# First period's rows from TensorE instead of DRAM, and the first slots regrouped by layer, in a CIN tower kernel

## The reference

```
x0 = e; xk = x0
for W in (W0, W1, W2):                       # W: (32, 32 or 64, 64)
    xk = relu(einsum('bmd,bhd,mhk->bkd', x0, xk, W))
    outs.append(sum(xk, axis=2))             # over d = 16
z = concatenate(outs, axis=1)                # (2048, 192)
h = relu(concatenate([z, dense_ctx]) @ W_top1 + b_top1)
h = relu(h @ W_top2 + b_top2)
y = h @ W_top3
```

## Time and profile before

| what | us |
|---|---|
| three timed runs, median | 655.9 |
| lowest and highest of them | 651.15, 657.07 |
| the profiled execution, own time | 651.37 |
| its span in the profile | 649.6 |

### The profile page before, as it was taken

One profiled execution on the slowest core, in us unless ns is written; L12 is line 12 of the kernel. 1 busy time (PEld: TensorE's weight loads), 2 busy tenths in 40 slices (PEclk: granted clock), 3 DMA queues, 4 the chain that ended last, 5 costly groups with the idle time before them and its releaser, 6 DMA issues.

```text
span 649.6 us, 7753 instructions
## 1 busy us (share of the span) xinstructions
PE 586.3 (90%) x2896; PEld 209.5 (32%) x2896; DVE 587.2 (90%) x327; ACT 358.4 (55%) x595; POOL 459.3 (71%) x381
## 2 busy tenths in 40 slices
PE   0078898999898989999999999999999999999997
PEld 0023332232232323333334323333334323333455
DVE  1038898999999999999999999999999999999993
ACT  0006382756646564757665465747576465736562
POOL 6676769588888888887989778887979692802020
PEclk9999999999999999999999999999999999999999
DMA  5285576728082644637280736546380816400000
GB/s 160 51 312 136 229 249 178 289 46 300 18 260 101 196 165 90 271 65 295 39 319 6 236 123 160 201 90 271 58 301 8 286 69 186 173 3 2 1 1 1
DMA packets 27137, 96.50 MB, mean 149 GB/s; under 512 B 7414, under 2 KB 12540, under 8 KB 22876
## 3 DMA queue, kind: packets, MB, share of 16 engines
q1 hardware_dynamic: 18908, 93.90, 43.2%
q0 software_dynamic: 8192, 2.11, 2.9%
HBM read 80.25 MB, written 15.73 MB: 148 GB/s over the span
## 4 chain that ended last, share of the span: by engine, by line
DVE 44%; PE 25%; issue 21%; POOL 4%; DMA 3%; SPq 1%; ACT 1%; another core or an unknown queue 0%; DVEq 0%; POOLq 0%
DVE prod L482 43%; PE acca L575 11%; PE accb L575 6%; PE acc L545 4%; POOL emb L361 3%; PE spread L616 2%; POOL prod L379 1%; SPq L279 1%; DMA emb<-in_table,idx 1%; DVE za L486 1%; DMA field_dram<-zb_field 1%; DMA rows<-field_dram 1%; DMA h<-in_w_swapped 0%; DVE zc L486 0%; PE spread L611 0%
## 5 line engine op out<-in xcount | busy, mean ns | idle before, releaser
L361 POOL DMA_INDIRECT emb<-in_table,idx x256 | 246.6, 963 | 82.2 <-issue 68.6
L575 PE MATMUL acca<-prod,w 128*64 128x512 f32 x1024 | 229.7, 594 | 4.1 <-DVE prod L482 2.8
L575 PE MATMUL accb<-prod,w 128*64 128x512 f32 x960 | 216.7, 596 | 15.9 <-DVE prod L482 12.0
L379 POOL TENSOR_TENSOR prod<-rows,mates 128x1024 f32<-128x1024 f32 x70 | 164.2, 2377 | 15.6 <-issue 15.2
L482 DVE TENSOR_TENSOR prod<-rows,x1a 128x2048 f32<-128x2048 f32 x64 | 145.9, 2282 | 5.4 <-PE acca L575 2.8
L482 DVE TENSOR_TENSOR prod<-rows,x1b 128x2048 f32<-128x2048 f32 x64 | 145.9, 2282 | 3.2 <-PE acca L575 1.9
L482 DVE TENSOR_TENSOR prod<-rows,x2b 128x2048 f32<-128x2048 f32 x64 | 145.9, 2282 | 1.3 <-remote 1.3
L482 DVE TENSOR_TENSOR prod<-rows,x2a 128x2048 f32<-128x2048 f32 x64 | 145.9, 2282 | 1.1 <-PE accb L575 0.8
L575 PEld LDWEIGHTS acca<-prod,w 128*64 128x64 f32 x1024 | 71.9, 137 | 147.0 <-issue 136.1
L575 PEld LDWEIGHTS accb<-prod,w 128*64 128x64 f32 x960 | 65.5, 137 | 158.6 <-issue 123.6
L709 ACT ACTIVATE x1a<-acc 64x512 f32<-64x512 f32 x62 | 35.3, 570 | 124.6 <-PE acc L545 103.4
(11 more groups left out here) (72 smaller groups left out, 251.4 us busy)
## 6 DMA issues: line engine op xcount, KB each, us to landing
rows<-field_dram SPq DMA_DIRECT2D x30, 2048.0 KB
field_dram<-zb_field SPq DMA_DIRECT2D x32, 256.0 KB
mates<-field_dram SPq DMA_DIRECT2D x16, 512.0 KB
emb<-in_table,idx POOLq DMA_INDIRECT x256
field_dram<-zb_field SPq DMA_DIRECT2D x32, 128.0 KB
field_dram<-zb_field SPq DMA_DIRECT2D x16, 192.0 KB
rows<-field_dram SPq DMA_DIRECT2D x2, 1024.0 KB
rows<-field_dram SPq DMA_DIRECT2D x1, 1536.0 KB
```

The source lines that it names most:

```text
L361: pool.indirect_dma_start(out=emb[q % EMBS][:, j * EMB:(j + 1) * EMB], out_offset=None, in_=table, in_offset=bass.IndirectOffsetOnAxis(ap= ...
L379: nc.gpsimd.tensor_tensor(prod0[:, (q * L0 + k) % RING0, :], rows[:, slot(q, t), :], mates[:, :], ALU.mult).then_inc(s_prod0p, 1)
L575: mm = nc.tensor.matmul(acc[j % 2][side * HID:(side + 1) * HID, :], (w1 if layer == 1 else w2)[:, step, :], prod[:, (made(layer, s, half, ...
```

## The change

Period 0 no longer goes through DRAM. VectorE first makes a pick matrix out of the identity (`pick`, in the space of `h2`). After the turn, ScalarE and VectorE copy the fields from PSUM into the lower 64 partitions of `field0`, and VectorE copies these to the upper 64. TensorE then forms the mates and each row tile by two matmuls (`pick_tile`), one for each half of the columns of the period, one from the lower and one from the upper 64 partitions; ScalarE copies them to `rows` and `mates` (VectorE half of the mates). Mates and tiles 0 to 4 come ahead of layer 0, tiles 5 to 7 behind it. The first five slots have new streams; slots 0 to 3 hold both subs of one layer of one period. In slots 0, 2 and 4 the last two units are made in halves. VectorE makes layer 0 of period 1 within slot 1, and the first two products of period 2 behind slot 2. The turns of periods 1 and 2, the sums of layer 0, GpSimd's gathers and the `keep_busy` calls are placed anew.

```diff
-    FIRST = [(0, 2), (2, 2), (4, 1), (5, 3)]
+    PICKED = [MATES, 0, 1, 2, 3, 4, 5, 6, 7]
+    EARLY = [[(1, 0), (1, 1)], [(2, 0), (2, 1)], [(1, 2), (1, 3)], [(2, 2), (2, 3)], [(1, 4), (1, 5)]]
     def streams(j):
-        if j == 0:
-            return [(1, 0), (1, 1)]
+        if j < len(EARLY):
+            return EARLY[j]
...
+    def feeds(j):
+        return j in (0, 2, 4)
     def vector_units(j):
         a, b = streams(j)
-        if 1 <= j < SUBS - 1:
+        if len(EARLY) < j < SUBS - 1:
             a, b = b, a
-        if j == 1:
+        if j in (1, 3, 5):
             return [(*stream, half, u) for half in range(2) for stream in (a, b) for u in range(UNITS)]
...
-    FIELDS_AT = {(0, 3): 2}
-    SUM0 = {}
+    FIELDS_AT = {(0, 0): 1, (0, 3): 2}
+    SUM0 = {(1, 1): [(k, 1) for k in range(L0)], (2, 3): [(k, 2) for k in range(L0)]}
-    def on_vector(q):
-        return q < 2
+    def on_vector(q, k):
+        return q < 2 or q == 2 and k < 2
...
 # SyncE
-            list_fields(0)
-            mates_in(0)
-            for g, (t, count) in enumerate(FIRST):
-                spread_rows(0, t, count, s_first[g])
 # GpSimd
-            gather_early(0)
+            gather(0, 0, GATHERS)
+            gather(1, 0, 2)
             pool.wait_ge(s_turned, 1)
-            gather_early(1)
-            pool.wait_ge(s_l0, L0)
-            gather_early(2)
-            gather_early(3)
+            gather(1, 2, 4)
+            pool.wait_ge(s_picked, 4)
+            gather(1, 6, 5)
+            pool.wait_ge(s_l0, 3)
+            gather(1, 11, 5)
+            gather(2, 0, 5)
+            pool.wait_ge(s_used, pairs_of(0, 0, 0))
+            gather(2, 5, 4)
+            pool.wait_ge(s_used, pairs_of(0, 0, 1))
+            gather(2, 9, 4)
+            pool.wait_ge(s_used, pairs_of(0, 1, 0))
+            gather(2, 13, 3)
+            gather(3, 0, STRETCH)
             halve12(0)
...
-            for k in range(L0):
+            gather(4, 0, STRETCH)
+            for k in range(2, L0):
                 product0(2, k)
...
 # VectorE
+            for c in range(2):
+                for j, count, half, first, step, times in LIST_PARTS:
+                    part = c * HID * P + c * HID + half * FIELDS + 2 * j + c
+                    ones_of = bass.AP(ident[:, :].tensor, part, [[P, HID], [0, times], [2, count]])
+                    to = bass.AP(h2[:, :, :].tensor, c * HID * TOP2 * 2 + 8 * first, [[TOP2 * 2, HID], [8 * step, times], [1, count]])
+                    last = nc.vector.tensor_scalar_max(to, ones_of, 0.0)
+            dve.wait_ge(s_turned, 1)
+            for d in (2, 3):
+                for f in range(2):
+                    last = nc.vector.tensor_copy(field0_at(f, d), turned_at(f, d))
...
+            nc.vector.tensor_copy(field0[HID:P, :], field0[0:HID, :]).then_inc(s_field0v, 1)
+            dve.wait_ge(s_picked, 1)
+            nc.vector.tensor_copy(mates[:, HALF:N], picked_at[0][1][:, :]).then_inc(s_matesv, 1)
...
+                    if (j, i) == (1, 5):
+                        for k in range(L0):
+                            product0(1, k)
+                if j == 2:
+                    for k in range(2):
+                        product0(2, k)
 # TensorE
+            def pick_tile(n):
+                first = PICKED[n]
+                for c in range(2):
+                    part = slice(c * HID, (c + 1) * HID)
+                    mm = nc.tensor.matmul(picked_at[n][c][:, :], pick[part, first:first + P], field0[part, :], start=True,
+                                          stop=True)
+                mm.then_inc(s_picked, 1)
+            pe.wait_ge(s_w12, 32)
+            pe.wait_ge(s_gather[0], SOON * 16)
+            keep_busy(acc[1][:, :], 5)
             turn_fields(0, 0)
...
+            for n in range(1 + L0):
+                if n >= 3:
+                    pe.wait_ge(s_copied, n - 2)
+                    pe.wait_ge(s_matesv, 1)
+                pick_tile(n)
...
-            turn_fields(1, 0)
-            keep_busy(acc[1][:, :], 5)
+            for n in range(1 + L0, len(PICKED)):
+                pe.wait_ge(s_copied, n - 1 if n == len(PICKED) - 1 else 1 + L0)
+                pick_tile(n)
+            keep_busy(spread[:, :], 3)
 # ScalarE
-            fields_out(0)
+            for d in (0, 1):
+                for f in range(2):
+                    last = nc.scalar.activation(field0_at(f, d), turned_at(f, d), ACT.Copy)
+            last.then_inc(s_field0, 1)
+            for n in range(1 + L0):
+                rows_out(n)
             input1(0, 0)
             input1(1, 0)
-            fields_out(1)
+            for n in range(1 + L0, len(PICKED)):
+                rows_out(n)
             input1(0, 1)
             input1(1, 1)
+            fields_out(1)
             z1(0)
...
-            input2(0, 0)
-            input2(0, 1)
-            input1(2, 0)
-            fields_out(2)
-            input1(2, 1)
-            z1(1)
-            z2(0)
-            z2(1)
+            for s in range(2):
+                input2(s, 0)
+            for s in range(2):
+                input2(s, 1)
+            z2(0)
+            z2(1)
+            fields_out(2)
+            for half in range(2):
+                input1(2, half)
+                input1(3, half)
```

More of the change, by code:

```diff
@@ L468, in product0, with outer @@
                                         ALU.mult).then_inc(s_prod0v, 1)
-            def outer(layer, s, half, u):
+            def outer(layer, s, half, u, part=None):
                 n = made(layer, s, half, u) - 1
                 q, c = s // 2, s % 2
+                if part == 1:
+                    outer_tiles(n, layer, s, half, u, QUADS // 2, QUADS // 2).then_inc(s_prod, 1)
+                    return
                 if (layer, half, c) == (1, 0, 0):
@@ L509, in _ @@
             for j in range(SUBS):
-                for i, unit in enumerate(vector_units(j)):
-                    outer(*unit)
+                units = vector_units(j)
+                for i, unit in enumerate(units):
+                    if feeds(j) and i == len(units) - 2:
+                        for part in range(2):
+                            for last_unit in units[-2:]:
+                                outer(*last_unit, part)
+                    elif not feeds(j) or i < len(units) - 2:
+                        outer(*unit)
                     if j % 2 == 1:
@@ L743, in input2 @@
                 act.wait_ge(s_used, taken(1, s, 1, UNITS - 1))
[L744 to L745 removed]
+                act.wait_ge(s_prod, made(*ahead(2, s), half, UNITS - 1))
                 if half == 0:
@@ L796, in tower_step, with rows_out @@
                 done.then_inc(s_act, 1)
-            fields_out(0)
+            def rows_out(n):
+                act.wait_ge(s_picked, n + 1)
+                if n == 0:
+                    last = nc.scalar.activation(mates[:, 0:HALF], picked_at[0][0][:, :], ACT.Copy)
+                else:
+                    for c in range(2):
+                        last = nc.scalar.activation(rows[:, slot(0, PICKED[n]), c * HALF:(c + 1) * HALF],
+                                                    picked_at[n][c][:, :], ACT.Copy)
+                last.then_inc(s_copied, 1)
@@ new lines, in _ @@
+            for half in range(2):
+                input1(2, half)
+                input1(3, half)
+            z1(1)
+            z3(0)
+            z3(1)
+            fields_out(3)
+            for half in range(2):
+                input2(2, half)
+                input2(3, half)
+            z2(2)
+            z2(3)
+            for half in range(2):
+                input1(4, half)
+                input1(5, half)
+            z1(2)
+            z3(2)
+            z3(3)
+            fields_out(4)
```

191 lines of the change are left out of this document (114 added, 77 removed).

## The result

| | before | after |
|---|---|---|
| runs on one chip, median (four each) | 655.8 us | 668.3 us |
| lowest and highest | 651.15, 657.07 | 667.23, 672.18 |
| profiled execution, span | 649.6 | 667.3 |

The changed kernel is slower, ratio 1.0252 with a 95% interval of 1.0194 to 1.031; 647.9 us was forecast. The same kernel repeated later (e5) took 657.4 against 649.3, ratio 1.0117 (1.0082 to 1.0152), and once more on another chip (e14) 667.0 against 651.2, 1.0222 (1.0147 to 1.0297). So there are two things to explain: 8 us that are lost in every set of runs, and 5 to 8 more that come in some.

The account below looks back on a forecast made before the run. VectorE was taken as the bound from 170.64 us, with the winnable time in the serial start. 10.1 (start) + 8.2 - 7.2 (waits) - 3.25 (work) = 7.9, said as 8, from the 655.9 median: 647.9 us, range 641 to 655.

Parts of the forecast that it names:

- (a) to (f): Steps of the start: warm-up, field copies, picks, PSUM copies, last product, late tiles; first outer product 10.1 us earlier.
- (e): Start's end: last layer-0 product, 1.22 us, then 2.46 to the first outer product, put at 39.4.
- rival A: Start: picks do not overlap and take 1.71 us each; gain only 4 us, 651.9; chance 0.13.
- The work term: First slots: VectorE gains two products of period 2, 2.35 us, and halved units, 0.9; together 3.25 us.
- the sum of waits: VectorE's idle time in the first slots: feeds, buffer waits and a gap, together 7.2 us.
- The prediction's own sign of being wrong: VectorE waiting more than 10 us in all between its first outer product and slot 6.
- The turn of period 2: TensorE, ahead of slot 1's outer unit 0: holds until the gathers have landed at 67.8; no VectorE wait counted.
- That fits with a few tenths: Slot 1: outer unit 0, queued behind period 2's turn, returns by 71.8, when VectorE needs it.
- rival B: First slots: late gathers delay period 2's turn and outer unit 0; 4 us late leaves gain 4, 651.9; chance 0.20.
- The feeds: VectorE's waits at slots 0 to 1, 2 to 3 and 4 to 5: 3.3, 1.0 and 1.0 us.
- The small waits: VectorE: 1.7 us for product buffers, mainly slots 1 and 3, and a gap of 0.2 before late tiles.
- The forecast that GpSimd ends the products of period 3 near 130: GpSimd, ahead of slot 5: gathers of period 4 no longer held, two products fewer; end at 130 instead of 149.9.

Follow-up runs that it names:

- e5: The changed kernel again, no edit, against the kernel before, signals on time: 657.4 us against 649.3, ratio 1.0117.
- e14: The changed kernel once more, no edit, against the kernel before, on another chip with late signals: 667.0 us against 651.2, ratio 1.0222.
- e6: Changed kernel with the turn of period 2 moved from behind slot 0's last contraction to behind slot 1's second: 658.0 us, ratio 1.0139.
- e11: Changed kernel with SyncE issuing period 1's mates and rows only once the fields of period 2 are turned: 655.8 us.
- e9: e7's edits on the changed kernel, plus five filler matmuls ahead of each pause in slots 2 and 4: 650.3 us, ratio 1.0011.
- e10: The picks alone, with slots, streams and places of work as in the kernel before: 646.0 us against 649.6, ratio 0.9947.
- e7: Changed kernel with turns of periods 2 and 3 later, fillers ahead of picks and more behind slot 0, period 1's gathers behind the turn: 651.8 us, ratio 1.0026.
- e18: Changed kernel with GpSimd's gathers of period 2 held back until slot 0 is through, on a chip with late signals: 683.0 us, ratio 1.0505.
- e12: e10 with period 1's turn behind slot 0's first pair and its first-layer products behind two units of slot 1: 665.3 us, ratio 1.0191.
- e15: e10 repeated, the picks alone against the kernel before, on another chip with late signals: 660.5 us against 652.5, ratio 1.0136.
- e17: e12's kernel with slot 1's four layer 2 units ahead of its four of layer 1, a repeat on another chip: 678.5 us, ratio 1.0408.
- e1: Changed kernel with all of GpSimd's gathers of period 1 moved behind the turn of period 0: 656.2 us against 649.1.
- e2: Changed kernel with GpSimd's gathers of period 2 held until slot 0's last contraction is done, signals on time: 670.2 us.

## Why the prediction was wrong

Against the steps, with e5 (signals on time) and the first profile after:

| step | forecast | e5 | first |
|---|---|---|---|
| turn's signal | 25.8 | 25.74 | 29.04 |
| fields ready | 27.7 | 27.56 | 30.69 |
| last copy ahead of layer 0 | 35.6 | 36.2 | 40.5 |
| first outer product | 39.4 | 40.67 | 44.93 |
| work added in slots 0 to 5 | 3.25 | 3.3 | 3.2 |
| idle of VectorE there | 7.2 | 20.8 | 25.1 |
| slot 5 begins | 143 | 155.6 | 163.9 |

**Right in mechanism.** (a) to (f) hold within 1.3 us where the signal is on time ((e) adds up to 39.3, not 39.4). The picks overlap (rival A fell); a pick is 0.86 us at full clock and 1.70 at half clock, where TensorE had stood 5.20 us before them (2.02 in e5, where about the first pick and a half are slow; 2.06 in e6, where none is). The copies of 128x512 are spaced at 0.5 and not 0.57, and take up part of it. The gathers beside the 64x512 copy of VectorE kept their rhythm of 1.25 us in e5, so nothing was owed there. The work term was right.

**The step that failed is the sum of waits**, 7.2, measured 20.8 in e5 and 25.1 in the first profile. The prediction's own sign of being wrong was more than 10. Its terms in e5:
- The turn of period 2, put at nothing. "That fits with a few tenths" took the last gather, issued at about 66, to have landed at 67.8. The issue time was right (66.73), the landing was not: the turn begins 7.3 us after it, since 4.5 MB of rows and mates, issued at 61.0 to 61.4, move beside it (e11: 2.4 without them). VectorE pays 4.97. This is rival B, with the transfer as its cause, which the text did not name. In the trace of before the turn of period 2 did not show it: it stood behind layer 0 of period 1 and began at 77.69, 8 us after the last gather's issue at 69.55. The change took that cover away. The turn of period 3, though, showed it in that same trace (SyncE's queue, GpSimd, TensorE):

```profile
89.14 0.91 SPq L293 DMA_DIRECT2D rows<-field_dram  x2
...
96.74 0.94 POOL L361 DMA_INDIRECT emb<-in_table,idx  x1 [0.30 <-issue]
...
102.97 0.68 PE L539 MATMUL spread<-ident,emb 128*32 128x128 f32 x16 [2.82 <-DMA emb<-in_table,idx]
```

  The last gather of period 3 was used 6.2 us after its issue, beside period 2's rows. So the price could have been read before the change. The Trainium skill, DMA: Bandwidth & Descriptors, Queues, rings and completion order, says that a DMA's semaphore increment lands only after every earlier write of the same DMA engine, across its queues. The traces agree: in e5 the DMA engines are full from 62 to 74 us and 9% busy from 74 to 76, and the turn begins at 74.05. No run tells this rule from the queues' merely sharing the DMA engines.
- The feeds, put at 3.3, 1.0 and 1.0: 4.6, 1.6 and 1.9. At 0 to 1 TensorE has more left than the 8 passes counted: its last 16 run from 59.52 to 63.12, 3.3 us beyond VectorE's end at 59.78; then ScalarE's first copy, from 63.22 to 64.37.
- The small waits, put at 1.9: 7.5, nine of them between 0.2 and 1.2. TensorE takes two units at a time, and in slots 1, 3 and 5 the order by stream completes its first pair only with the third unit. It stands for 3.6 to 4.1 us ahead of slots 3 and 5, the granted clock is then at half for some 3.5 us at a time, and VectorE waits for product buffers. By e9 the clock is a part of this; that the order is the rest is argued, not shown.

The sum, by e5 against the profile of before: 8.9 won, 20.8 - 8.15 = 12.6 more idle, 3.3 more work: 7.0 lost, spans 656.6 and 649.6. e10 bounds the parts from the other side: without the new slots the gain is 3.6 us. e7 does too: with both turns moved (and the fillers) the loss falls from 8.0 to 2.5 us.

**The rest of the first result**, 667.3 against 656.6, is in no step: 4.3 us at the start (the signal 3.3 later, and the picks at half clock up to 36.6), 5.8 more in slot 0 (24.9 against 19.1), 2.1 behind slot 5, less 1.5 in between. e18 ties the late signals to gathers in flight. Late signals were in the trace before as well, where they cost little; ScalarE's timeline there, with the turn's end at 50.24:

```profile
52.48 1.53 ACT L704 ACTIVATE zb_field<-spread 32x256 f32<-32x256 f32 x4 [1.90 <-remote]
```

Why these signals are late, why in some sets only (the chip and the time of the runs changed together, though one chip was on time twice), and why the kernel before loses less by them (its medians are 649.1 to 649.6 in the sets on time, 650.0 to 652.5 in the others and 655.8 in the first) stays open. The forecast that GpSimd ends the products of period 3 near 130 missed too: in e5 they run from 122.99 to 139.6.

## What to carry to other kernels

- A wait for gathers, in an in-order queue, is to be costed with whatever bulk transfer runs beside them: 2.4 us from issue to use without one, 7.3 with one. Look for the same wait elsewhere in the trace of before, in a place where nothing covers it (6.2 us for period 3). Put nothing urgent behind it, or move every such wait, since moving one only hands the delay to the next (e6, e7).
- When a start is shortened, ask what the old first slots covered. Here DRAM's trip for the second period was covered by work that now starts 9 us earlier; with signals on time the picks alone kept 3.6 of 9 us, and reordering the slots for the rest cost 11.
- One chip's result is not the result: repeat the pair on another before its size is explained. One and the same kernel, the picks alone, won on one chip (0.9947) and lost on another (1.0136).

## What was not expected of the hardware

- TensorE's signal for a turn reached waiting engines 2.2 to 12.0 us after its last matmul (in e12, 27.72 after 25.54 and 67.69 after 55.72), in four sets of runs (the first, e12 to e14, e15 to e17, e18), with gathers by indirect DMA in flight; in e1 to e11 it came at once (turn's end 25.68, copies at 25.74 in e5).
- Beside 4.5 MB of row transfers the last gather was used 7.3 us after its issue (e5), 6.9 in e1 and 6.2 in the kernel before; without them 2.4 to 2.6 (e11, e2).
- Two contractions of 64 rows, on the upper and the lower half of the array, each fp32 in two passes, take 0.86 us together at a granted clock of 1.00 (2.4 GHz) and 1.70 at 0.50 (1.2 GHz).
